# A four-layer decoder on one core: the mixer's turned tiles go by DMA transposes in place of TensorE, and the mixer's steps take another order

## What is computed

```python
u_n = layer_norm(u, ln_w, ln_b)
proj = jnp.einsum('bsd,ed->bse', u_n, in_proj_w)      # z 1024 | x 1024 | B 128 | C 128 | dt 16
B, C = rms_norm(B, bnorm_w), rms_norm(C, cnorm_w)
y = ssd_chunked(x, softplus(dt + dt_bias) * A, B, C, CHUNK)
y = (y + x * D).reshape(b, s, D_INNER) * jax.nn.silu(z)
return u + jnp.einsum('bse,de->bsd', y, out_proj_w)
```

## Time and profile before

| what | before |
|---|---|
| median of 3 runs | 1072.49 us (1072.23 to 1072.78) |
| profiled execution, its own time | 1071.19 us |
| span of that execution, first to last instruction | 1069.5 us |
| granted TensorE clock, mean | 0.995 |
| busy: PE, DVE, ACT, POOL | 1027.0, 827.4, 622.3, 448.0 us |
| chain that ended last, by engine | PE 69%, DVE 14%, ACT 6%, POOL 5%, issue 5% |

### The profile page before, as it was taken

The page is one execution under the profiler, slowest core; times in us unless marked ns, Lnnn a source line. Parts: engine busy times, 40 slices in busy tenths (PEclk is TensorE's granted clock), DMA queues, the critical chain, the costliest instruction groups (busy, mean ns, idle before and its releaser), DMA issues.

```text
span 1069.5 us, 15247 instructions
## 1 busy us (share of the span) xinstructions
PE 1027.0 (96%) x5121; PEld 762.7 (71%) x5121; DVE 827.4 (77%) x1751; ACT 622.3 (58%) x1209; POOL 448.0 (42%) x655
## 2 busy tenths in 40 slices
PE   7899999999999999899999999999899999999998
PEld 6677788778877887766567787877676666666544
DVE  6597757776777667846988868786888989989975
ACT  5643344444443433336566557764578989989784
POOL 3334324332333223425988552005564654745521
PEclk9899999999999999999999999999999999999999
DMA  8411111000111111317110036410001111112123
GB/s 295 156 58 64 36 46 37 25 27 36 41 40 40 41 40 40 121 24 304 65 40 1 2 121 258 148 45 1 1 6 24 43 34 39 42 35 52 34 57 77
DMA packets 49261, 69.37 MB, mean 65 GB/s; under 512 B 33056, under 2 KB 34336, under 8 KB 44832
## 3 DMA queue, kind: packets, MB, share of 16 engines
q1 hardware_dynamic: 49184, 68.40, 19.6%
HBM read 56.69 MB, written 4.33 MB: 57 GB/s over the span
## 4 chain that ended last, share of the span: by engine, by line
PE 69%; DVE 14%; ACT 6%; POOL 5%; issue 5%; DVEq 0%; ACTq 0%; POOLq 0%
PE bank L444 50%; PE bank L528 5%; PE bank L452 4%; PE bank L915 3%; PE bank L539 2%; PE bank L519 2%; PE bank L458 2%; POOL dt L2333 1%; DVE ctx_lo L1272 1%; PE bank L495 1%; DVE wgt L1035 1%; DVE eu L1233 1%; DVE at L1535 1%; ACT squares L2159 1%; DVE prod L1523 1%
## 5 line engine op out<-in xcount | busy, mean ns | idle before, releaser
L444 PE MATMUL bank<-win_hi,a_uT_hi 128*128 128x512 f32 (+1 forms) x320 | 126.5, 395 | 3.7 <-DVE win_lo L992 2.5
L444 PE MATMUL bank<-win_lo,a_uT_hi 128*128 128x512 f32 (+1 forms) x320 | 120.1, 375 | 0.0
L444 PE MATMUL bank<-win_hi,a_uT_lo 128*128 128x512 f32 (+1 forms) x320 | 119.6, 374 | 0.0
L1752 ACT ACTIVATE x<-x,a_rs 128x512 f32<-128x512 f32 x16 | 12.8, 813 | 120.1 <-DVE un L971 120.1
L2357 POOL TENSOR_TENSOR y<-y,off 128x512 f32<-128x512 f32 x24 | 33.8, 1409 | 98.7 <-DVE off L1054 98.7
L444 PEld LDWEIGHTS bank<-win_hi,a_uT_hi 128*128 128x128 f32 x320 | 60.5, 189 | 17.5 <-DVE win_lo L992 4.0
L444 PEld LDWEIGHTS bank<-win_lo,a_uT_hi 128*128 128x128 f32 x320 | 60.5, 189 | 12.5 <-issue 2.4
L444 PEld LDWEIGHTS bank<-win_hi,a_uT_lo 128*128 128x128 f32 x320 | 60.4, 189 | 10.9
L528 PEld LDWEIGHTS bank<-xs,wgt 128*128 128x128 f32 x512 | 62.6, 196 | 6.8 <-issue 5.5
L1795 ACT ACTIVATE zs<-bank 128x512 f32<-128x512 f32 x32 | 19.1, 598 | 79.2 <-PE bank L444 79.2
L444 PE MATMUL bank<-f,fqT_next 128*128 128x512 fp8e4 (+1 forms) x312 | 64.0, 362 | 0.0
(11 more groups left out here) (342 smaller groups left out, 3075.7 us busy)
## 6 DMA issues: line engine op xcount, KB each, us to landing
cum_all<-cum_rows SPq DMA_DIRECT2D x16, 1024.0 KB, 4.7
wchunk<-w_in SPq DMA_DIRECT2D x32, 256.0 KB, 6.3
stage<-f_in SPq DMA_DIRECT2D x3, 1408.0 KB, 6.1
x<-x_in SPq DMA_DIRECT2D x16, 256.0 KB, 5.6
land<-win_in SPq DMA_DIRECT2D x4, 1024.0 KB, 7.8
wq<-ctxT_in SPq DMA_DIRECT2D x4, 1024.0 KB, 6.5
out<-x SPq DMA_DIRECT2D x16, 256.0 KB, 2.0
ctx<-ctx_in SPq DMA_DIRECT2D x3, 1024.0 KB, 4.9
```

Of the source, the lines that this page charges most:

```text
L444: made = e.matmul(bank, a, b, start=start and n == 0, stop=stop and n == len(pairs) - 1)
```

## The change

Tiles 3 to 15 of `un` and tiles 0 to 14 of `y` are turned by DMA. A 32-bit number is taken as two 16-bit numbers. A copy on ACT (`split_un`, `split_y`) lays the low and the high halves of a row into two planes. SP writes the planes to device memory (256 KB, `un_rows` and `y_rows`), waits until they are there, and issues a DMA transpose of the 256 x 512 16-bit matrix back into the tile itself, so that the halves lie side by side again. The readers take the turned tile from SBUF in place of PSUM. The planes of `un` lie on the ring of `a_uT_lo`, those of `y` on `zs`. TensorE still turns tiles 0 to 2 of `un` and tile 15 of `y`. Every engine's list for a round has another order, and SP's loop goes by rounds with the turns ahead of and behind `spread_cum`. Waits that counted TensorE's turns are renumbered, in the later layers too.

```diff
+FIRST_TURNS, LAST_TURN = 3, NT - 1
...
+        lo_start = ph.at
+        a_uT_lo = ph.ring("a_uT_lo", 2, [P, KD, P], F32R)
+        un_planes = Region(nc, lo_start, ph.at).ring("un_planes", 2, [P, 2, D], U16)
...
+        un_rows = nc.dram_tensor("un_rows", (NT, P, 2, D), U16)
+        y_rows = nc.dram_tensor("y_rows", (NT, 2, P, 2, 512), U16)
...
+        def halves_of(ap):
+            return ap.bitcast(U16).rearrange("p (d t) -> p t d", t=2)
+        def planes_in(ap):
+            return ap.bitcast(U16).rearrange("p (t d) -> p t d", t=2)
+        def y_planes(k, n):
+            return planes_in(zs[k % 2][:, n * 512:(n + 1) * 512])
+        def turned_halves(ap):
+            return ap.bitcast(U16).rearrange("p (k r) -> p k r", r=2 * P)
+        def turned_y(k, n):
+            return banks.of["yT", k, n][:] if k == LAST_TURN else y[k % 2][:, n * 512:(n + 1) * 512]
...                                                    # TensorE, a round
-                if new:
-                    project(i, 0)
                 if mix:
                     turn_bc(m)
-                if i + 1 < NT:
-                    turn_un(i + 1)
-                if old:
-                    turn_y(k, 0)
+                if k == LAST_TURN:
+                    turn_y(k, 0)
+                if new:
+                    project(i, 0)
                 if mix:
                     pair(m)
+                if k == LAST_TURN:
+                    turn_y(k, 1)
                 if new:
                     project(i, 1)
+                if i + 1 < FIRST_TURNS:
+                    turn_un(i + 1)
+                if new:
                     project(i, 2)
                 if mix:
                     off_product(m, 0)
+                    off_product(m, 1)
                 if new:
+                    sums(i)
                     running(i)
-                    sums(i)
-                if old:
-                    turn_y(k, 1)
+                    project(i, 3)
                 if mix:
                     y_product(m, 0)
-                if new:
-                    project(i, 3)
+                if mix:
+                    y_product(m, 1)
                 if new:
                     project(i, 4)
-                if mix:
-                    off_product(m, 1)
-                    y_product(m, 1)
...                                                    # VectorE
             def scale_un(i):
-                bank = banks.of["un", i]
+                bank = un if i >= FIRST_TURNS else banks.of["un", i]
                 w.wait_ge("ln_loaded", 32)
-                w.wait_ge("u_turned", i + 1)
+                if i >= FIRST_TURNS:
+                    w.wait_ge("un_back", 16 * (i - FIRST_TURNS + 1))
+                else:
+                    w.wait_ge("u_turned", i + 1)
...
-                e.tensor_tensor(yT_lo[:, cols], banks.of["yT", k, n][:], yT_hi[:, cols].bitcast(F32),
+                e.tensor_tensor(yT_lo[:, cols], turned_y(k, n), yT_hi[:, cols].bitcast(F32),
...                                                    # ScalarE
+            def split_un(i):
+                if i < FIRST_TURNS:
+                    return
+                w.wait_ge("u_ready", i + 1)
+                w.wait_ge("projected", 5 * (i - 1))
+                e.activation(un_planes[i % 2][:], halves_of(un[:]), ACT.Copy).then_inc(sig("un_split"), 1)
+            def split_y(k, n):
+                w.wait_ge("y_gated", 2 * k + n + 1)
+                e.activation(y_planes(k, n), halves_of(y[k % 2][:, n * 512:(n + 1) * 512]), ACT.Copy).then_inc(
+                    sig("y_split"), 1)
...
             def tanh_z(i, n):
                 w.wait_ge("projected", 5 * i + 4 + n)
                 if i >= 2:
-                    w.wait_ge("y_gated", 2 * (i - 2) + 2)
+                    w.wait_ge("y_out", 32 * (i - 1))
...
             def high_yT(k, n):
-                w.wait_ge("y_turned", 2 * k + n + 1)
+                if k == LAST_TURN:
+                    w.wait_ge("y_turned", n + 1)
+                else:
+                    w.wait_ge(f"y_back_{n}", 16 * (k + 1))
...                                                    # GpSimd, skip_y
-                    w.wait_ge("y_turned", 2 * (m - 2) + 2)
+                    w.wait_ge("yT_lo", 2 * (m - 2) + 2)
...                                                    # SyncE
+            def turn_un(i):
+                if i < FIRST_TURNS:
+                    return
+                w.wait_ge("un_split", i - FIRST_TURNS + 1)
+                e.dma_start(un_rows.ap()[i], un_planes[i % 2][:]).then_inc(sig("un_out"), 16)
+                w.wait_ge("un_out", 16 * (i - FIRST_TURNS + 1))
+                e.dma_start_transpose(turned_halves(un[:]), un_rows.ap()[i].rearrange("p t d -> (p t) d")).then_inc(
+                    sig("un_back"), 16)
+            def turn_y(k, n):
+                w.wait_ge("y_split", 2 * k + n + 1)
+                e.dma_start(y_rows.ap()[k, n], y_planes(k, n)).then_inc(sig("y_out"), 16)
+                w.wait_ge("y_out", 16 * (2 * k + n + 1))
+                e.dma_start_transpose(turned_halves(y[k % 2][:, n * 512:(n + 1) * 512]),
+                                      y_rows.ap()[k, n].rearrange("p t d -> (p t) d")).then_inc(sig(f"y_back_{n}"), 16)
...
-            for i in range(NT):
-                spread_cum(i)
+            spread_cum(0)
+            load_x(1)
+            for i in range(1, NT + 2):
+                m, k = i - 1, i - 2
+                new, mix, old = i < NT, m < NT, 0 <= k
+                if i + 1 < NT:
+                    turn_un(i + 1)
                 if i < BATCH - 1:
                     load_x(i + 1)
+                if new:
+                    spread_cum(i)
+                if m < LAST_TURN:
+                    turn_y(m, 0)
+                    turn_y(m, 1)
```

More of the change, by code:

```diff
@@ L1192, in vector_program @@
                 if mix:
-                    gate_y(m, 0)
-                if new:
-                    gate_z(i, 0)
-                if mix and new:
-                    weigh_pair(m, 3)
-                if old:
-                    low_yT(k, 1)
+                    scale_off(m, 0)
+                if old:
+                    low_yT(k, 0)
+                    low_yT(k, 1)
+                if mix:
+                    gate_y(m, 0)
+                    scale_off(m, 1)
+                if i + 1 < NT:
+                    low_uT(i + 1)
+                if i == 1:
+                    normal(3)
                 if i > 1 and i + 3 < NT and (i + 3) % TPB == 0:
@@ L2433, in gpsimd_program @@
                 new, mix = i < NT, m < NT
[L2434 to L2435 removed]
+                if i > 2 and i + 2 < NT and (i + 2) % TPB == 0:
+                    stats((i + 2) // TPB + 1)
+                if i == NT:
+                    mean_u(0)
                 if mix and i > 1:
```

196 lines of the change are left out of this document (107 added, 89 removed).

## The result

The changed kernel takes 1039.14 us (median of 4 runs, 1038.63 to 1039.42) against 1072.36 of the kernel before in the same comparison (4 runs, 1071.21 to 1072.78). The ratio is 0.9689, with a 95% interval of 0.9674 to 0.9705. That is 33.2 us less where 13.8 were forecast. The profiled execution took 1039.38 us, with a span of 1037.3 against 1069.5 and a mean granted clock of 0.998 against 0.995.

What follows compares the result with a forecast made beforehand. TensorE's own instructions were taken to bound the mixer. Transposes saved 18.7 us, waits added 4.9: -13.8 from the profiled 1071.2 gives 1057.4, plus 1.3 for the runs' median 1058.7, rounded to 1058.5; range asked for 1053 to 1076.

Steps and rivals of the forecast that it cites:

- The bound: In the mixer, TensorE's own instructions set the pace; DVE is next, 6.8 us a tile behind.
- The transposes, 18.7 us: Mixer, TensorE: removing 13 tiles of un at 0.44 us and 28 halves of y at 0.465 saves 18.7 us.
- Waits ahead of the pair, 4.9 us: Mixer: TensorE waits for cT ahead of the pair, 1.5 us a sequence net, 4.9 us over 13 tiles.
- the walk: A middle mixer tile's steps placed in the new lists, on earlier durations; its round took 27.1 us.
- Split 1.05 to 1.15: ACT, three times a tile: copying 1024 16-bit numbers takes 1.05 to 1.15 us, upper end 2.1.
- The transpose from device memory, 3.1 us: DMA turns of un and y: a 256 x 512 transpose, eight blocks, lands after 3.1 us.
- The end of 6 us: Upper end for the DMA transpose's landing: 6 us if a source in device memory costs as much again.
- `scale_un` waits from 7.0 to 9.2 and costs 0.8: Middle tile, DVE: scale_un waits for un's turned rows from 7.0 to 9.2, then costs 0.8 instead of 1.3.
- Three meetings of DVE and POOL, 3.2 us: Middle tile: three DVE steps with both inputs in SBUF wait for POOL, 3.2 us, where two cost 2.0.
- In the middle tiles I expect none of it: Mixer's middle tiles: no fall of TensorE's clock, though it may fall where TensorE starts to wait.
- the rival's price: Late un rows at scale_un: landing at 4.7 under 0.1 a tile, then 1 us per us on 13 tiles; 0.18 beyond 6.
- the sum -18.7 + 4.9: Whole kernel: transposes saved less waits added, -13.8 us; a forecast near 1058.5 had chance 0.55.

Runs made afterwards that it cites:

- e1: The changed kernel with its new lists, but TensorE turns all tiles of un and y, none by DMA: 1062.98 us.
- e6: The changed kernel, but all halves of y are turned by TensorE, un still by DMA: 1054.7 us.
- e5: The changed kernel, but all 16 tiles of un are turned by TensorE, y still by DMA: 1045.05 us.
- e13: The changed kernel with one further, unused copy of 512 numbers (0.6 us) on ACT behind split_un each round: 1043.31 us.
- e4: The changed kernel with the order of before in rounds 1 and 2 alone, DMA turns kept: 1053.32 us.
- e9: The changed kernel with all the old lists in round 1 only: 1053.12 us.
- e11: The changed kernel with only ACT's old list in round 1: 1049.85 us.
- e12: The changed kernel with the old lists in rounds 16 and 17, the end of the mixer: 1045.02 us.
- e8: The changed kernel with the planes of un written to device memory three times before the turn, rows 4.2 us later: 1094.55 us.

## Why the prediction was wrong, step by step

- **The bound: right.** TensorE sets the pace, and it does so after the change too (26.30 busy in a tile of 26.30).
- **The transposes, 18.7 us: right in size, in part by luck.** The middle region lost 19.9, with 18.3 of transposes in it. But e1 against the changed kernel puts only 16.4 us on the turns, since `y`'s brought less than their starts say (10.1 of 13.0 by e6, while `un`'s 5.7 are met by e5). The other 3.5 are the new order's, which the sum had at nothing; the waits for POOL in the earlier trace rows (1.4 us), gone in e1 too, are a part of them.
- **Waits ahead of the pair, 4.9 us: wrong, 1.0 came.** The prediction had 0.7 us in two tiles of a sequence, 0.35 in the third and none in the first. The chip had 0.22 to 0.37 in the last tiles of the sequences (3, 7 and 11), 0.22 in tiles 2 and 14, and none in the others. One cost was mis-sized that I can name. I counted the two squares of B and C as 0.98 us of ACT, adding the durations on the rows (an activation and a read of its sum, twice). They overlap, and by their starts they take 0.50. The kernel before shows it, in its timeline of ACT:

```profile
203.14 0.25 ACT L1769 ACTIVATE bs<-bank 128x128 f32<-128x128 f32 x1
203.30 0.19 ACT L1769 ACTIVATION_READ_ACCUMULATOR bs<-bank 128x1 f32 x1
203.39 0.26 ACT L1769 ACTIVATE cs<-bank 128x128 f32<-128x128 f32 x1
203.55 0.20 ACT L1769 ACTIVATION_READ_ACCUMULATOR cs<-bank 128x1 f32 x1
203.64 1.14 ACT L1821 ACTIVATE wgt<-wgt 128x512 f32<-128x512 f32 x2
```

That is the rule that I had used for TensorE, starts and not durations, and not kept on ACT. The changed kernel, timeline of ACT, from the split to the fourth exponential:

```profile
185.37 1.06 ACT L1796 ACTIVATE un_planes<-un 128x1024 uint16<-128x1024 uint16 x1 [5.63 <-DVE un L999]
186.33 0.26 ACT L1817 ACTIVATE bs<-bank 128x128 f32<-128x128 f32 x1
...
191.06 1.28 ACT L1869 ACT_TABLE_LOAD   x1
...
194.09 0.61 ACT L1869 ACTIVATE wgt<-wgt 128x512 f32<-128x512 f32 x1
```

  The stretch takes 9.33 us (185.37 to 194.70), and about 10.0 in the walk. But e13 put 0.6 us back and paid only 0.09 a tile, so the squares carry a part at most. The rows show the rest: the split starts 1.84 after `turn_bc` (185.37 - 183.53) where the walk had 2.9, so the walk was 1.1 us late before ACT began. From there its round was nearly right: from one `cT` to the next it had 27.0 us, and 26.84 passed (184.87 to 211.71). What was wrong, as far as the rows show, is that the walk let this longest round follow on itself and so began it late. In the tile before, DVE still waited 0.64 us for TensorE ahead of `add_mixed` (182.08), so it starts tile 6 on time. Only behind the next round is it late, by 0.22 us, and it has caught up in the first tile of the next sequence.
- **Split 1.05 to 1.15: right.** 1057 ns, 0.96 between starts.
- **The transpose from device memory, 3.1 us: right.** It landed after 3.3, the write after 2.0. The DMA issues on the page, to be set beside the earlier trace rows:

```profile
y_rows<-zs SPq DMA_DIRECT2D x30, 256.0 KB, 2.0
...
un_rows<-un_planes SPq DMA_DIRECT2D x13, 256.0 KB, 2.0
...
y<-y_rows SPq DMA_TRANSPOSE x30, 3.3
...
un<-un_rows SPq DMA_TRANSPOSE x13, 3.3
```

  The end of 6 us for a source in device memory didn't come. The Trainium skill ("DMA: Bandwidth & Descriptors", Why small descriptors are slow), which I had cited, says that small packets lose bandwidth on device memory. Here at most 0.2 us of that shows, 3.3 against the 3.1 that I had from the sources in SBUF.
- **`scale_un` waits from 7.0 to 9.2 and costs 0.8: right in kind.** The wait is 2.45 us, it costs 1.03 from its start to the next, and the rows are there 8.3 us after `turn_bc` (191.79 - 183.53). The timeline of DVE in the changed kernel:

```profile
185.25 0.87 DVE L1066 TENSOR_SCALAR wgt<-cum_all,neg 128x128 f32<-128x128 f32 x4
...
191.79 1.11 DVE L1010 TENSOR_SCALAR un<-un,lnw,lnb 128x128 f32<-128x128 f32 x4 [2.45 <-DMA un<-un_rows]
...
194.74 0.69 DVE L1073 TENSOR_TENSOR wgt<-wgt,cb 128x512 f32<-128x512 f32 x1 [0.64 <-ACT wgt L1869]
...
195.95 2.36 DVE L1137 TENSOR_TENSOR yT_lo<-y,yT_hi 128x512 fp32r<-128x512 f32 x2
...
202.84 1.66 DVE L1100 TENSOR_TENSOR y<-y,zs 128x512 f32<-128x512 f32 x1
204.42 2.51 DVE L1066 TENSOR_SCALAR wgt<-cum_all,neg 128x128 f32<-128x128 f32 x4
206.86 1.21 DVE L1115 TENSOR_TENSOR state<-state,ex 128x1024 f32<-128x1024 f32 x1
```

  The last weighing ends at 195.43, 11.9 after `turn_bc`, where the walk had 13.5. TensorE begins the y products at 12.7 (196.25), where the walk had 13.4, its own wait of 0.7 included. The walk had the order right and DVE 1.6 us too late here: 1.1 from the start of the round, and 0.65 from ACT's stretch.
- **Three meetings of DVE and POOL, 3.2 us: nearly right in size (3.7), one of them unforeseen.** `low_yT` takes 2.36 for two (1.28 at 246.92, where POOL has no step beside it) and `gate_y` 1.66 (0.69). The third isn't `decay_state` (1.21, undisturbed) but four clamps, 2.51 in place of 0.87. A clamp reads one tile and one number a partition, so by my rule of "both inputs in SBUF" it should have been free. POOL's `skip_y` runs beside it:

```profile
203.91 2.36 POOL L2411 TENSOR_TENSOR y<-xs,dvec 128x1024 f32<-128x1024 f32 x1
```

  The Trainium skill, "GPSIMD Engine Reference", 1. Specifications, names two kinds of DVE instruction that contend with GpSimd: those with two SBUF inputs, and those in a mode that uses both ports, which "VectorE: DVE Perf Modes", Mode 2×_2P, gives to a single-source step from SBUF. The trace agrees, with 0.87 alone and 2.51 beside POOL; in which mode the clamps ran, it doesn't show.
- **The start, which isn't in the sum at all: the largest miss, 9.5 us.** The prediction read TensorE's waits from 93 us on and took the first tile of the mixer for one of its middle tiles. The wait of 3.94 us at 40.6 and the lower level behind it stood in the trace. A changed order in every list changes round 1 too, and e4 and e9 to e11 show that it is there that the order pays most.
- **The clock.** "In the middle tiles I expect none of it": right for the changed kernel. It is wrong in the rival's price, where late turns pull the clock down with them, and the start has no term for the 3.4 us that the clock cost there.
- **The end.** 3.1 us less where nothing was counted; open, as said under e12.

In short, what failed is the sum -18.7 + 4.9. The 4.9 came as 1.0, the order's 3.5 in the middle tiles and the 9.5 of the start had no term, and neither had the 3.1 of the end, whose cause is open.

## What to carry over

When a change reorders every engine's list, walk the first and the last round as well as a middle one, and read the waits of the bounding engine over the whole stage. Distances between starts come nearer to the price than durations, on ACT's small steps too, though the turns of `y` brought even less than that (10.1 of 13.0 us). Don't let the longest round of a repeated group of tiles follow on itself: walk the group. And trace a kernel more than once before a difference of a few us is given a cause, since the same kernel ran from 1038.6 to 1044.4 us. Two edits that each move a different limit (TensorE's work, and the round through the other engines) don't add: here the one alone gave 9.4, the other nothing, and both 33.2.

## What the hardware showed that I hadn't expected

- A wait of TensorE can cost more than its length: behind 3.94 us of waiting stood 6.8 us at half the clock, 3.4 us more. In e8, with single waits of up to 4.3 us, the mean stood at 0.93 over 355 us. The same waits need not cost the same: behind 0.73 and 1.5 us ahead of the same steps stood 3.4 us at the lower level in the changed kernel and 13.6 in e13.
- A DVE step that reads one SBUF tile (four clamps of 128 x 128) went from 0.87 to 2.51 us beside POOL, more than a step with two inputs (0.69 to 1.66).
- A DMA transpose of 256 x 512 16-bit numbers from device memory took 3.3 us to land, 0.2 more than the 3.1 that the two sizes from SBUF in the earlier trace rows let expect.
